# A decoder of two layers on one core: the order of ScalarE's exponentials, VectorE's inverses and GpSimd's products where causal pairs are woven with heads

## What is computed

```python
# layer 1, causal attention: 16 heads of 64 channels
scores = where(tril, einsum('biph,biqh->biqp', K, Q), -1e10)
attn = softmax(scores / sqrt(64), axis=-1)
z = einsum('biph,biqp->biqh', V, attn)
out = einsum('bqf,df->bqd', z_flat, W_O)
# layer 1, cross attention on the context: 16 heads of 8 channels
scores = einsum('bhqd,bhkd->bhqk', qh, kh) * 8 ** -0.5
attn = softmax(scores, axis=-1)
out = einsum('bhqk,bhkd->bhqd', attn, vh)
```

## Time and profile before

| | |
|---|---|
| Median of 3 runs | 822.47 us (820.80 to 823.44) |
| The profiled execution's own time | 822.54 us |
| Its span in the profile | 820.7 us |
| Mean granted TensorE clock | 0.929 |
| TensorE busy (matmul) | 726.9 us, 89% of the span |
| TensorE weight loads | 539.3 us, 66% |
| VectorE | 483.8 us, 59% |
| ScalarE | 420.1 us, 51% |
| GpSimd | 290.1 us, 35% |

### The profile page before, as it was taken

The page is one execution under the profiler, slowest core; times in us unless marked ns, Lnnn a source line. Parts: engine busy times, 40 slices in busy tenths (PEclk is TensorE's granted clock), DMA queues, the critical chain, the costliest instruction groups (busy, mean ns, idle before and its releaser), DMA issues.

```text
span 820.7 us, 16176 instructions
## 1 busy us (share of the span) xinstructions
PE 726.9 (89%) x5744; PEld 539.3 (66%) x5744; DVE 483.8 (59%) x1293; ACT 420.1 (51%) x1062; POOL 290.1 (35%) x400
## 2 busy tenths in 40 slices
PE   5559899899898998999999989979889888999886
PEld 2336576675665665899898977657556555667666
DVE  3457697876957776444543455545544449675652
ACT  2115458666576677754544467454554545454311
POOL 0013365555645666310000046232143435444300
PEclk7659799999999999999999999999988798899999
DMA  7553353533628273000000000000000015000000
GB/s 235 171 122 79 81 118 68 131 78 82 133 54 205 64 202 105 2 1 1 2 1 1 1 1 3 1 26 16 24 18 3 19 53 197 18 2 8 8 7 7
DMA packets 25174, 48.10 MB, mean 59 GB/s; under 512 B 7264, under 2 KB 14192, under 8 KB 25096
## 3 DMA queue, kind: packets, MB, share of 16 engines
q1 hardware_dynamic: 24376, 45.66, 22.1%
q10 hardware_dynamic: 720, 1.41, 0.5%
HBM read 17.49 MB, written 0.52 MB: 22 GB/s over the span
## 4 chain that ended last, share of the span: by engine, by line
PE 62%; DVE 16%; ACT 9%; issue 8%; DMA 2%; POOL 1%; SPq 1%; POOLq 0%; DVEq 0%; ACTq 0%
PE G L580 8%; PE SC L837 7%; PE SC L824 7%; PE SC L767 5%; PE G L621 4%; ACT causal_probs L1151 3%; PE SC L860 3%; DVE shift_cols L1530 3%; PE SC L739 3%; PE G L935 3%; PE SO L890 3%; PE SO L810 2%; PE G L585 2%; DVE negmax L1538 2%; ACT exps L1166 2%
## 5 line engine op out<-in xcount | busy, mean ns | idle before, releaser
L1530 DVE TENSOR_REDUCE shift_cols<-SC 128x2 f32<-128x512 f32 x192 | 130.6, 685 | 64.6 <-PE SC L739 62.7
L1166 ACT ACTIVATE exps<-SC 128x512 f32<-128x512 f32 x192 | 114.4, 596 | 99.7 <-PE SC L767 99.2
L1608 POOL TENSOR_TENSOR rstd<-variance,consts 128x2 f32<-128x2 f32 (+1 forms) x48 | 37.2, 775 | 294.0 <-DVE variance L1230 291.1
L1140 ACT ACTIVATE hidden<-SC,cols 128x256 f32<-128x256 f32 x128 | 53.5, 470 | 65.1 <-PE SC L824 64.9
L1151 ACT ACTIVATE causal_probs<-SC,negmax 128x128 f32<-128x128 f32 (+1 forms) x128 | 52.1, 423 | 53.0 <-DVE negmax L1538 52.8
L1699 POOL TENSOR_TENSOR causal_probs<-causal_probs,inverse 128x256 f32<-128x256 f32 x64 | 51.6, 826 | 56.2 <-DVE inverse L1543 56.2
L1564 DVE SCALAR_TENSOR_TENSOR R<-SC,small,R 128x128 f32<-128x128 f32 x128 | 39.0, 346 | 53.9 <-PE SC L837 53.3
L837 PEld LDWEIGHTS SC<-ffn_w,hidden 128*128 128x128 f32 x512 | 66.0, 192 | 5.3 <-issue 1.8
L767 PE MATMUL SC<-stacked_q,stacked_k 100*128 100x256 f32 x256 | 66.3, 342 | 3.3 <-DMA stacked_q<-shift_rows 1.7
L739 PE MATMUL SC<-stacked_k,stacked_q 96*128 96x256 f32 x256 | 56.5, 307 | 14.0 <-DMA stacked_q<-q_lo 6.9
L837 PE MATMUL SC<-ffn_w,hidden 128*128 128x128 f32 x512 | 67.6, 276 | 0.0
(11 more groups left out here) (254 smaller groups left out, 1551.8 us busy)
## 6 DMA issues: line engine op xcount, KB each, us to landing
stacked_k<-k_hi SPq DMA_DIRECT2D x64, 128.0 KB, 2.4
stacked_q<-q_hi SPq DMA_DIRECT2D x64, 128.0 KB, 2.4
ffn_w<-in_ffn_w SPq DMA_DIRECT2D x16, 512.0 KB, 4.9
stacked_k<-k_lo SPq DMA_DIRECT2D x32, 128.0 KB, 2.4
stacked_q<-q_lo SPq DMA_DIRECT2D x32, 128.0 KB, 2.4
packed_k<-U SPq DMA_DIRECT2D x48, 32.0 KB, 1.9
packed_q<-YN SPq DMA_DIRECT2D x48, 32.0 KB, 1.9
a_weights<-in_a_li SPq DMA_DIRECT2D x3, 256.0 KB, 7.8
```

The lines of the kernel that those rows point to most:

```text
L1140: last = fn(hidden0[i % 4][:, f, :], g[:, f * T:(f + 1) * T], ACT.Gelu, bias=col("ffn0_b1", 2 * e + f))
L1166: fn(exps[:, n % EXPS, :, :].rearrange("p t q -> p (t q)"), turned_bank(n).rearrange("p t q -> p (t q)"), ACT.Exp, scale=ATTENTIONS[LX]["s ...
L1530: v.tensor_reduce(shift_cols[:, n // UNIT % 4, :, n % UNIT], score_bank(n), axis=AX.X, op=ALU.max, negate=True).then_inc(head_max, 1)
```

## The change

Three calls are moved, for pairs 18 to 31 only (`pair_of(...) >= ALONE`). ScalarE's `pair_exponentials(i)` goes from `front` to `back` of the pair's slot: behind the side steps, `sums_drawn`, the head's exponential and `first_guess`, and ahead of the copies of transposed probabilities and of outputs. VectorE's `pair_inverses(i)` goes from `front` to the head of `back` in the slot after, behind the side steps. GpSimd's `normal_probs(i)` goes from `front` to the end of `back` in the slot after, behind the side steps and `check_inverse`. No instruction is added or taken away, and the order on TensorE and SyncE is as before.

```diff
--- before.py
+++ after.py
@@ -1179,7 +1179,7 @@
                         gelu_up(slot - M0_AT)
                     if slot == L1_AT:
                         nc.scalar.preload_act_table_set(EXP_AND_LN)
-                    if pair_of(slot) is not None:
+                    if pair_of(slot) is not None and pair_of(slot) < ALONE:
                         pair_exponentials(pair_of(slot))
 
                 def back(slot):
@@ -1189,6 +1189,8 @@
                         head_exponential(head_of(slot - SHIFT_LAG))
                     if unit_of(slot, INVERT_AT) is not None:
                         first_guess(unit_of(slot, INVERT_AT))
+                    if pair_of(slot) is not None and pair_of(slot) >= ALONE:
+                        pair_exponentials(pair_of(slot))
                     i = pair_of(slot - LAG)
                     if i is not None:
                         copied(("PT", i, 1), PT[:, i % TURNED, 1, 0:3 * P], lambda g: g[:, 0:3 * P])
@@ -1572,10 +1574,12 @@
                         head_maximum(head_of(slot))
                     if pair_of(slot) is not None:
                         pair_maxima(pair_of(slot))
-                    if pair_of(slot - 1) is not None:
+                    if pair_of(slot - 1) is not None and pair_of(slot - 1) < ALONE:
                         pair_inverses(pair_of(slot - 1))
 
                 def back(slot):
+                    if pair_of(slot - 1) is not None and pair_of(slot - 1) >= ALONE:
+                        pair_inverses(pair_of(slot - 1))
                     if unit_of(slot, REFINE_AT) is not None:
                         refine(unit_of(slot, REFINE_AT))
                     if unit_of(slot, DIVIDE_AT) is not None:
@@ -1713,6 +1717,8 @@
                 def back(slot):
                     if unit_of(slot, INVERT_AT) is not None:
                         check_inverse(unit_of(slot, INVERT_AT))
+                    if pair_of(slot - 1) is not None and pair_of(slot - 1) >= ALONE:
+                        normal_probs(pair_of(slot - 1))
 
                 through_slots(front, sides(linear, nothing, nothing, after, nothing, settle, nothing, causal_out, nothing, nothing,
                                            mix), back)
```

## The result

The changed kernel took **831.13 us** (median of 4 runs, 827.11 to 833.78) against 821.63 us for the kernel before (4 runs, 820.69 to 823.44): a ratio of 1.0109, 95% interval 1.0056 to 1.0161. It is 1.1% slower; forecast were 819.9 us and a range that ended at 823.4. The profiled execution took 829.0 us, its span 827.2 (before 820.7), at a mean granted clock of 0.915 (before 0.929).

What follows compares the result with a forecast made beforehand. TensorE was taken as the bound, idling 8.2 us for head exponentials because of ScalarE's order. Sum: 822.54 - 2.5 + 0.8 + 0.25 - 1.15 = 819.9 us, range 816.3 to 823.4.

Steps and rivals of the forecast that it cites:

- Pairs 23 and 25: Head's exponential ahead of the pair's; transposes, bound by the shift copy, start 0.67 us earlier in each pair.
- Pair 24: Head's exponential ahead of the pair's, with no shift copy there: 1.15 us off its period of 6.28 us.
- Copy of XN: In slot 226 this copy goes ahead of pair 21's exponentials, so TensorE's draw starts earlier: 1.15 us off.
- The costs: Pairs 27, 29, 31 wait for a late head's product, 0.8 us on; pairs 26, 28, 30 together 0.25 us on.
- the term for the clock: The sum assumes as many low stretches of TensorE's clock as today, so nothing is added for them.
- The third rival: Slower: low clock meets the slots of pairs 27, 29, 31, whose late product delays the pair's exponentials; 825.1 us, chance 0.1.
- Its price for such a slot: At low clock in a units' values slot, the late head's product makes the transposes 1.3 us late.
- Its price per microsecond: From a single matmul: a 6.8 us low-clock stretch would take 4.6 us at the high clock, 2.1 us a stretch.
- Slot 221: Copy of drawn queries goes ahead of pair 18's exponentials; cover 0.3 us, price up to 0.5, taken as nothing.
- Inverses and products: VectorE's inverses and GpSimd's products at the back stay off the path: no term, covered by 2.4 us.
- The other two rivals: One or two low clock stretches go, 817.8 or 815.6 us; or waits move on, 822.7 us; chance 0.2 each.
- the late bank: Rival: TensorE, let go earlier, meets the same late bank at transposes or keys' copy; 822.7 us, chance 0.2.

Runs made afterwards that it cites:

- e7: The whole change plus eight useless products on TensorE ahead of the waiting transposes behind pairs 25, 27, 29 and 31: 814.68 us, 0.9873 of the kernel before.
- e5: All three moves for pairs 18 to 26, 28 and 30 only; 27, 29 and 31 as in the kernel before: 818.66 us, 0.9946 of it.
- e6: All three moves for pairs 18 to 25, 27, 29 and 31 only; 26, 28 and 30 as in the kernel before: 829.66 us.
- e10: The kernel before plus eight useless products ahead of the waiting transposed product behind pairs 25, 27, 29 and 31: 818.33 us, 0.9975 of the kernel before.
- e8: The whole change, with the exponentials of pairs 21, 23, 25, 27, 29 and 31 further back, behind the shift copy: 811.72 us, 0.9803 of the kernel before.
- e4: All three moves for pairs 26 to 31 only; pairs 18 to 25 as in the kernel before: 835.38 us, 1.0206 of it.
- e3: All three moves for pairs 18 to 25 only; pairs 26 to 31 as in the kernel before: 820.93 us, 0.9965 of it.
- e9: The kernel with exponentials behind the shift copy, those of pairs 26, 28, 30 also behind the unit's sums' copies: 805.70 us, 0.9781 of the kernel before.
- e11: The whole change plus eight useless products behind, not ahead of, the transposes after pairs 25, 27, 29 and 31: 825.99 us, 1.0025 of the kernel before.
- e2: Only VectorE's inverses and GpSimd's products moved back; ScalarE's order as in the kernel before: 824.88 us, 1.0014 of it.
- e1: Only ScalarE's pair exponentials moved behind the head's, from pair 18 on; otherwise the kernel before: 833.56 us, 1.0131 of it.

## Why the prediction was wrong

**The terms of the order held.** Pairs 23 and 25: 0.67 us each foretold, 0.61 (6.27 to 5.66) and 1.11 (6.77 to 5.66, of which some is clock) measured. Pair 24: 1.15 foretold, 1.56 measured (6.28 to 4.72). Copy of XN: 1.15 foretold, 1.44 measured (7.80 to 6.36). Together 3.65 against 4.72. The costs: pair 27 at the high clock takes 6.51 instead of 6.28 us, 0.23 against the 0.15 foretold. For pairs 26 to 30 at the high clock together, the new order's periods are 10.64, 6.51, 8.01, 6.51 and 6.90 us (e7, the change, e5, e6, e7), 38.6 in all, and the old order's 10.70, 6.28, 7.67, 6.28 and 6.94 (e10, and pairs 27 and 29 of before), 37.9. The new order costs 0.7 us there by itself; I had 1.05 with pair 31.

**The step that failed is the term for the clock, put at nothing by the half sentence "with the clock's low stretches as many as today".** As many they were: three before and three after. But the sum takes from it that the time at the low clock stays, and it grew: 6.8, 6.8 and 13.6 us became 10.2, 17.1 and 17.1. From the same sums, the clock cost pairs 26 to 30 45.18 - 37.9 = 7.3 us before and 53.29 - 38.6 = 14.7 after. Those 7.4 us are most of the error of 9.1 (829.0 in the profiled execution against 819.9), and the runs show the cause by what ends it: with products added where TensorE waits (e7) the clock of that stretch is 0.96 and the kernel takes 814.68 us, with the same order of ScalarE. The account of the two profiled spans: -2.46 up to pair 18's scores (VectorE, ScalarE and their order are the same there; the clock is 0.93 before against 1.00 between 477 and 500 us; no moved call stands there, so this part is luck of the execution), -3.26 for pairs 18 to 25, +8.11 for 26 to 30, +4.1 from pair 31 on: +6.5.

**The third rival had the direction, but not the way.** It foretold slower by the low clock, with a chance of 0.1. Its condition was that both pair 27 and pair 29 run at the low clock. Pair 27 did not: from 617.76 to 624.27 the clock is 1.00, and its period 6.51. Only pair 29 starts at the low clock and takes 9.06 us. Its price for such a slot was right: behind pair 31, at the low clock, the transposes start 2.68 us after the head's product is done (661.57 to 664.25), where it was 1.26 before (659.18 to 660.44), so 1.42 us later against the 1.3 foretold. What it had too small is the added low clock: 6.8 us more of it, where the stretch of pairs 26 to 30 alone had 18 us more (39 against 22). Its price per microsecond was too small as well. The 301 matmuls of that stretch are busy for 31.88 us at clock 1.00 (e8), 41.08 with 22 us at the low clock and 49.17 with 39, which makes 2.9 us for 6.8 us of low clock and not 2.1, the number taken from a single matmul.

**Where the reasoning could have found it.** I had the chain: at the low clock ScalarE's work starts from a later product while it keeps its pace. I used it for the length of a slot, and didn't ask what it does to TensorE's idleness. The row of 660.01 in the trace of before shows the old wait shrunk to 0.47 us at the low clock, where it is 1.67 at the high one. In the new order the two waits of such a slot are 0.43 and 1.42 us behind pair 29 and still 0.22 and 1.42 behind pair 31 (0.22 and 1.14 in e4). That the waits keep most of their size stands in these rows; that this is why the low clock lasts is only argued, and the rows within the middle low stretch, e3, e9 and e11 speak against its being the whole of it. The 2.67 us of idleness in pair 25 went as the prediction had it, with 0.43 and 1.58 us left one instruction later (0.5 and 1.5 foretold).

**Slot 221 was foretold at nothing** and pair 18 took 8.63 instead of 7.23 us. Not by its order: the clock stood at 0.50 there, in this window of the changed kernel:

```profile
546.00:552.80 6.80, 6.80 (x29) 5.14 (x30) 2.49 (x5) 0.34 (x1) 1.61 (x2) 0.50 0.20 53
```

e3, e5 and e6 have the same order and took 7.27, 7.23 and 7.18 us, while e2, with ScalarE in the old order, took 8.42. **Inverses and products** cost nothing, as foretold (e2).

The other two rivals: no low stretch went (three remain), and the late bank did not take the gains of pairs 23 to 25 away, since e1, e3, e5, e6 and e7 all keep them.

What stays open: why a given wait is followed by a low clock in one execution and not in the next (the 1.00 us behind pair 27 in e4 is followed by over 9 us at clock 1.00), why low stretches last 6.8 us in one place and 17 in another with TensorE busy throughout, and how far the tail behind pair 31, which varies between 166.3 and 176.9 us over the profiled kernels, answers to the change or to chance. It is longest in e1 and e4, which moved pair 31, and 166.3 to 169.4 in the five that left it in its place; but e7, which moved it, has 167.3.

## What to carry to other kernels

A move that shortens an engine's waits in one slot can cost more than it gains if TensorE's clock falls for longer behind it: here 4.7 us of gains against some 7 us of clock in five pairs. Look also at what the waits left over do when the clock is low: here the one that starts from TensorE's own last result kept most of its size, and the one that ends at a time set by ScalarE shrank from 1.67 to 0.47 us. The remedy that worked is to let the other engine free what the slow engine needs next (here the 0.36 us shift copy) ahead of the long work that nobody waits for yet. And when the clock is a suspect, adding useless products where TensorE waits is a quick test: if more work makes the kernel faster, as it did here, lateness is ruled out and the clock is what is left.

## What the runs showed of the hardware

Some 8.2 us of useless fp32 products made the changed kernel 2% faster (831.13 to 814.68 us, in two sessions, each beside the kernel before at 821.6 and 820.7). No wait in the stretch was longer than 1.6 us, and the clock was at 0.50 for most of it. The Trainium skill, page "TensorE: Matmul & The Clock Gate", section "A second HAM failure mode: psum-queue depth-cycling", tells of a kernel in which short pauses between groups of matmuls are enough to make the clock swing between its two levels. The trace agrees in that short waits went with two levels of the clock: 0.63 of full clock over 53.29 us with 4.12 us of idleness. It also shows low stretches without any pause in them, 15.80 us of matmuls without a gap at 0.50.

A product of 128 x 128 by 128 columns in fp32 shows as two instructions; eight of them took 2.05 us at the high clock (e7) and 3.62 us at the low one (e11).

VectorE's scaling of the residual, which ran beside nothing of GpSimd's in the kernel before, took nearly twice as long beside the moved products and the key sum behind them. The refinement, for which I had expected this, kept its 0.41 us. Lines of VectorE by form between 600 and 670 us (busy us, mean ns), before and then after:

```profile
L1241 DVE TENSOR_SCALAR X<-R,moments,rstd 128x128 f32<-128x128 f32 x2 | 0.6, 339 | 0.0
```

```profile
L1243 DVE TENSOR_SCALAR X<-R,moments,rstd 128x128 f32<-128x128 f32 x2 | 1.2, 645 | 0.0
L1549 DVE SCALAR_TENSOR_TENSOR unit_inverse<-unit_sums,unit_inverse 128x256 f32<-128x256 f32 x3 | 1.2, 414 | 0.0
```

It cost TensorE 0.5 us once (the wait of L518 above).
